# Eight gathers, one memset: how POOL closes a group of gathers in a two-layer graph network

## The reference

```python
h = relu(layernorm(x))
msg = sum over r of (h[src] * (edge_type == r)) @ L0_weight[r]      # 16 relations, 64 x 64
x = x + segment_sum(msg, dst)
h = relu(layernorm(x))
m = relu(concat([h[src], h[dst], edge_attr]) @ W1 + b1) @ W2 + b2   # 136 -> 64 -> 64
x = x + segment_sum(m, dst)
```

## Time and profile before

| | us |
|---|---|
| median of 3 runs | 4952.87 (4940.25 to 4954.87) |
| the profiled execution, its own time | 4951.48 |
| its span | 4949.3 |
| POOL busy | 3439.7 (69%) |
| PE busy | 2744.9 (55%) |
| DVE busy | 1470.4 (30%) |
| ACT busy | 582.2 (12%) |

### The profile page before, as it was taken

One profiled execution on the slowest core, in us unless ns is written; L12 is line 12 of the kernel. 1 busy time (PEld: TensorE's weight loads), 2 busy tenths in 40 slices (PEclk: granted clock), 3 DMA queues, 4 the chain that ended last, 5 costly groups with the idle time before them and its releaser, 6 DMA issues.

```text
span 4949.3 us, 40507 instructions
## 1 busy us (share of the span) xinstructions
PE 2744.9 (55%) x10310; PEld 1528.5 (31%) x10310; DVE 1470.4 (30%) x2002; ACT 582.2 (12%) x1139; POOL 3439.7 (69%) x6536
## 2 busy tenths in 40 slices
PE   2656555565565655566655454555555554555555
PEld 1434333343343333333422222222222222222222
DVE  6323222222222222222233332333233232332333
ACT  3111111111111111111110000000000000000000
POOL 7567676676776776676756676777777767767676
PEclk8777777777777767776766666666666666666666
DMA  4111111111111111111111111111111111111111
GB/s 100 21 25 25 27 25 24 24 27 24 25 27 25 25 27 25 24 27 24 25 29 29 29 29 30 29 30 31 29 31 31 29 29 30 29 30 32 28 30 26
DMA packets 391188, 144.16 MB, mean 29 GB/s; under 512 B 321650, under 2 KB 337323, under 8 KB 391163
## 3 DMA queue, kind: packets, MB, share of 16 engines
q0 software_dynamic: 106304, 109.07, 11.5%
q1 hardware_dynamic: 282245, 34.18, 4.8%
q10 hardware_dynamic: 2614, 0.62, 0.1%
HBM read 129.03 MB, written 12.83 MB: 29 GB/s over the span
## 4 chain that ended last, share of the span: by engine, by line
POOL 34%; issue 23%; another core or an unknown queue 21%; PE 12%; DVE 6%; DMA 2%; DVEq 1%; ACT 1%; POOLq 0%; ACTq 0%; SPq 0%
POOL rows L710 31%; PE ps L1462 3%; PE ps L1379 2%; PE ps L1461 2%; POOL spacer L743 2%; PE ps L1466 1%; DVE z_slot L1230 1%; DVE slots L1219 1%; DVE q_blk L1243 1%; DMA rows<-p_table,idx 1%; DVEq L1234 1%; POOL spacer L763 1%; PE ps L1386 1%; DMA rows<-h_table,idx 1%
## 5 line engine op out<-in xcount | busy, mean ns | idle before, releaser
L710 POOL DMA_INDIRECT rows<-p_table,idx x1661 | 1580.3, 951 | 728.9 <-issue 510.2
L710 POOL DMA_INDIRECT rows<-h_table,idx x1533 | 1451.9, 947 | 695.9 <-issue 417.5
L1379 PE MATMUL ps<-onehot,rows 128*64 128x256 f32 x3328 | 742.2, 570 | 500.6 <-DMA rows<-h_table,idx 407.2
L1461 PE MATMUL ps<-w_attr,attr_t 64*128 64x512 f32 x416 | 368.0, 980 | 1087.4 <-DVE q_blk L1243 753.8
L1095 DVE TENSOR_TENSOR onehot<-key,ps 128x2048 f32<-128x2048 f32 x209 | 473.9, 2278 | 532.0 <-remote 344.6
L1379 PEld LDWEIGHTS ps<-onehot,rows 128*64 128x64 f32 x3328 | 364.5, 199 | 787.4 <-issue 693.2
L1219 DVE TENSOR_TENSOR slots<-ps,rows 128x512 f32<-128x512 f32 x208 | 143.8, 692 | 1263.0 <-remote 698.4
L1386 PE MATMUL ps<-w_types,slots 128*128 128x128 f32 x3328 | 464.2, 297 | 86.6 <-issue 85.3
L1386 PEld LDWEIGHTS ps<-w_types,slots 128*128 128x128 f32 x3328 | 430.6, 209 | 163.7 <-issue 157.8
L1461 PEld LDWEIGHTS ps<-w_attr,attr_t 64*128 64x128 f32 x416 | 87.8, 262 | 1125.2 <-issue 1124.8
L1462 PE MATMUL ps<-q_blk,onehot 128*128 128x512 f32 x416 | 405.9, 1077 | 0.0
(11 more groups left out here) (142 smaller groups left out, 1939.3 us busy)
## 6 DMA issues: line engine op xcount, KB each, us to landing
rows<-p_table,idx POOLq DMA_INDIRECT x1661
rows<-h_table,idx POOLq DMA_INDIRECT x1533
attr<-in_edge_attr_dram SPq DMA_DIRECT2D x52, 128.0 KB
q_win<-q_table SPq DMA_DIRECT2D x208, 32.0 KB
p_table<-pq_out SPq DMA_DIRECT2D x25, 120.0 KB
q_table<-pq_out SPq DMA_DIRECT2D x25, 120.0 KB
out_dram<-xs SPq DMA_DIRECT2D x25, 120.0 KB
xs<-in_x_dram SPq DMA_DIRECT2D x6, 480.0 KB, 6.3
```

The source lines that it names most:

```text
L710: pool.indirect_dma_start(rows[:, u, t, :], None, table, bass.IndirectOffsetOnAxis(ap=at, axis=0)).then_inc(s, 16)
L1379: last = pe.matmul(slot_ps[t % 2 * D:(t % 2 + 1) * D, b, t // 2, :], rows[:, u, t, :], onehot[:, b, t, :], start=True, stop=True)
L1461: pe.matmul(pre_ps[:, u % 2, :], attr_t[half, u // 2, :], w_attr[half].rearrange("k j d -> k (j d)"), start=True, stop=False)
```

## The change

`spacer` grows from one row of 8 cells to 128 x 512. In both loops the memset moves out of the loop over the tiles: POOL issues the eight gathers back to back, then one memset over the whole of `spacer`, which raises `spaced` by one. The waits and the first increment count groups in place of tiles. No other engine's program changes.

```diff
-        spacer = sb("spacer", [1, T], fp32)
+        spacer = sb("spacer", [P, T * D], fp32)
...
-                pool.sem_inc(spaced, T)
+                pool.sem_inc(spaced, 1)
...
-                        wait_apart(pool, spaced, T * ((it - 2) * U + u + 1))
+                        wait_apart(pool, spaced, (it - 2) * U + u + 1)
...
                         for t in range(SKIP if last and u == U - 1 else 0, T):
                             gather(h_table, u, t, rows_in[u])
-                            pool.memset(spacer[:, t:t + 1], 0.0).then_inc(spaced, 1)
+                        pool.memset(spacer[:], 0.0).then_inc(spaced, 1)
...
-                        wait_apart(pool, spaced, T * ((NIT - 2 + it) * U + u + 1) - SKIP)
+                        wait_apart(pool, spaced, (NIT - 2 + it) * U + u + 1)
...
                         for j in range(SKIP if last and u == U - 1 else 0, T):
                             gather(p_table, u, j, rows_in[u])
-                            pool.memset(spacer[:, j:j + 1], 0.0).then_inc(spaced, 1)
+                        pool.memset(spacer[:], 0.0).then_inc(spaced, 1)
```

## The result

The kernel became faster, not slower: 4862.72 us (median of four runs, 4856.88 to 4865.98) against 4952.51 for the kernel before (four runs beside them, 4940.25 to 4954.87). The ratio is 0.982, with a 95% interval of 0.980 to 0.984. The forecast was 5001 us; its range ended at 4945.

What follows compares the result with a forecast made beforehand. The prediction took POOL's own gather pace to bound the kernel, 93% of the two loops. Longer heads, (42 + 70) x 0.44 = 49 us, with 0 for hidden memsets and stalls, made 4951.5 + 49 = 5001 us; range 4945 to 5070.

Steps and rivals of the forecast that it cites:

- POOL's own cost: At each group's head on POOL: one 128x512 memset of 0.53 us makes the head 1.49 us instead of 1.05.
- The upper bound of 0.69: Upper bound in us for POOL's 128x512 memset, from VectorE's tensor operation of that size; a head would gain 0.60 us.
- The small memsets hidden: Between POOL's gathers: one-cell memsets of 0.09 us run in the shadow of the gather's 0.30 us preparation; removing them gains 0.
- The stalls stay: Second gather of a turn's seventh group: 49 stalls of 0.83 us, up to 41 us if gone; counted as 0.
- The waits shrink: POOL's waits at group heads for PE or DVE to use group k-2: from 0.88 us less each in layer 0.
- POOL's own pace has the other 93%: Both loops, 4,681 us: waits for others beyond each head's ordinary 0.96 us are 347 us, 7%; POOL's pace is the rest.
- the heads that pay: Group heads not covered by waits: 42 in layer 0 and 70 in layer 1, at 0.44 us each, add 49 us.
- a slow sum of 11.6 us: Layer 0 on PE: one group's sum reached ACT after 11.6 us, the next, the same matmuls, after 3.4 us.
- All absorbed: Rival, chance 0.20: PE and DVE set the 94 us turn, POOL's 90.6 us still fit, time stays at 4951 us.
- Faster: Rival, chance 0.08: the 0.83 us stalls go with the shorter loop body and heads are absorbed, saving 41 us: 4910 us.
- Little absorbed: Rival, chance 0.10: PE starts later or runs at the lower clock, waits do not shrink; 270 heads give 5070, all 398 5127.
- at times slow: The prediction's description of PE behind POOL's layer 0 waits: one group's sum took 11.6 us, the next 3.4 us.

Runs made afterwards that it cites:

- the move alone: The kernel after, with a one-cell memset at each group's end in place of the 128x512 one: 4927.16 us, ratio 0.996 to the kernel before.
- The 128x64 memsets: The kernel before, with a memset of 128x64 in place of one cell behind each gather: 4929.64 us, ratio 0.996.
- the 768 columns: The kernel after, with a spacer of 128x768 instead of 128x512 in both layers: 4876.67 us, ratio 0.985 to the kernel before.
- a kernel with one group more of lead: The kernel after, with POOL waiting for group k-3 instead of k-2, on a faster chip: 4745.11 us, ratio 1.036 to the kernel before.
- the fastest version beside slow stretches: The kernel after with memsets of 128x768 in layer 0 and 128x512 in layer 1: 4848.50 us, ratio 0.979; on a faster chip 4785.91, ratio 1.045.
- the kernel without spacer: The kernel after without the memset, its semaphore and the wait for it: 4207.96 us, ratio 0.919, on a faster chip; 5144.47, ratio 1.038, on a slower one.

## Why the prediction was wrong, point by point

- **POOL's own cost: right.** Memset 0.54 us for 0.53; head 1.50 for 1.49; 0.96 us of idle time behind the memset; gathers 1.25 us apart with 0.30 idle. The own turn of 87.1 us held in layer 0 (87.0), layer 1's was 88.0. The upper bound of 0.69 was not needed.
- **The small memsets hidden: nearly right.** No gap changed. But the kernel with the move alone gained 0.4%, 18 us, where I had put 0; the interval excludes no change, and the cause is not known. The 128x64 memsets show where hiding ends: 0.17 + 0.16 is 0.03 above 0.30.
- **The stalls stay: right for this change,** 49 of them. That they come with the length of the loop's code was not shown; without the memset and its wait they are gone together with the heads' extra idle time.
- **The waits shrink: right in direction, wrong in size.** I expected each wait to shrink by the 0.88 us that two memsets add. Layer 1's went from 48 waits and 198.9 us to 4 and 10.7 us. Their excess over 1.05 was 3.5 us a head; 0.88 us can't remove that if the waited-for work keeps its length.
- **This is the step that failed: "POOL's own pace has the other 93%", and the waits as delays of a fixed size.** I counted the heads that wait, took from each what the pause could cover, and let the others pay 0.44 us. Such a sum can only end at zero or above. The consumer's pace was not fixed: PE and DVE needed 93 to 95 us a turn when they worked behind their data, and in layer 1 they kept up with 91 when they worked in step with them. So the term of 49 us for the heads that pay came out as a gain of 90. The three signs of it that I had (turns of equal length though the waits fall at different places, PE idle for 41% to 53%, a slow sum of 11.6 us beside a fast one of 3.4) I used as arguments for and against an absorbed cost, and did not ask whether the slow sums depend on POOL's pace, which the 768 columns show.
- **The rivals.** "All absorbed" had the right owner of the turn, PE and DVE, and the wrong constancy; it gave 4951, 88 us too much. "Faster" was to come from the stalls, which stayed: right in sign, by a mechanism that did not act. "Little absorbed" with all heads paying, 175 us, is close to what a chip without slow stretches shows (165.5 us for the same pause, in a kernel with one group more of lead), though not by the lateness of PE that the rival named.
- **What the row could have said.** The earlier trace rows is the row. A sum of the same 16 matmuls that takes three times as long, with a granted clock not lower than in the fast one, was no work of known size. I called PE "at times slow", took it as given and went on to count.

## What to carry to other kernels

If a producer waits for its consumers while no consumer is busy, the consumers' pace is the thing to measure: once with the producer far ahead (one buffer more), once in step. If they differ, a pause in the producer can pay for itself, up to the point where its own turn meets theirs. And measure a few per cent on several chips before they are built in: the same pause gave 1.6% to 1.9% in three comparisons, its like cost 3.6% in another, and the fastest version beside slow stretches was the slowest of all where there were none.

## What the runs showed of the hardware

- Chips differ in how fast PE delivers: the kernel before takes 4945 to 4956 us on some and 4580 and 4587 on two others, the kernel without spacer 5144 and 4208. Gathers cost the same 1.25 us on both kinds. (Or one chip differs from one time to another; none was visited twice.)
- On the slower kind the sum of eight tiles (16 matmuls of 128x256) has taken 11.6 us where 3.4 to 3.7 is usual, and the granted clock does not tell these stretches apart. The starts of the matmuls do: up to 2.8 us apart within one line in the kernel before, with no wait between them, and never over 1.1 on the faster kind.
- POOL's memset takes 89 ns for one cell, 168 for 128x64, 514 for 1x512, 542 for 128x512 and 756 for 128x768: the columns set it, the partitions hardly.
- A gather's preparation of 0.30 us hides a memset of 0.09 us wholly and one of 0.17 but for 0.03; a wait for POOL's own memset costs 0.96 us in place of these 0.30.
